# The attention readout's product with the context's low part, cut to two matmuls on 64 rows each

## The reference

```
x = x + xattn(layernorm(x), ctx, mask)
    scores = h @ ctx.T / sqrt(1024), masked; attn = softmax(scores)      # 64 columns
    out    = attn @ ctx                                                  # the readout, 64 x 1024
x = x + ffn(layernorm(x))
    base   = h @ weight.T                                                # 1024 x 1024
    router = softmax(h @ router_w.T), top 2 of 8 experts, renormalized
    out    = base + sum over experts of gate * (h @ lora_A.T) @ lora_B.T * 2
```

## Time and profile before

| | |
|---|---|
| median of 3 runs | 1096.29 us (1095.71 to 1096.64) |
| the profiled execution | 1095.92 us, span 1094.1 us, mean granted TensorE clock 0.994 of full |
| TensorE matmul busy | 1074.6 us, 98% of the span, 6240 matmuls |
| TensorE weight load busy | 1045.9 us, 96% |
| VectorE busy | 789.2 us, 72% |
| ScalarE busy | 466.5 us, 43% |
| GpSimd busy | 114.2 us, 10% |

### The profile page before, as it was taken

How to read it: one execution, slowest core, us unless ns; L and a number is a source line. 1 busy time by engine, 2 the same in 40 slices (tenths; PEclk the granted TensorE clock), 3 DMA queues, 4 the chain that set the end, 5 groups by cost and what they waited for, 6 DMA issues and landing times.

```text
span 1094.1 us, 18329 instructions
## 1 busy us (share of the span) xinstructions
PE 1074.6 (98%) x6240; PEld 1045.9 (96%) x6240; DVE 789.2 (72%) x2047; ACT 466.5 (43%) x954; POOL 114.2 (10%) x282
## 2 busy tenths in 40 slices
PE   7899999999999999999999999999999999999998
PEld 6799999999999999999999999999999999999998
DVE  5867867768677777677777677677776677776663
ACT  5643443443443443443533444434444434434330
POOL 2510010010010010110000100100100100100100
PEclk8999999999999999999999999999999999999999
DMA  9453534643535543544536434445435635345322
GB/s 323 112 164 116 154 84 129 183 136 116 153 81 161 153 123 127 142 115 137 153 105 173 129 95 142 134 147 151 117 95 153 163 116 154 78 133 154 92 64 78
DMA packets 70974, 145.89 MB, mean 133 GB/s; under 512 B 8848, under 2 KB 44176, under 8 KB 70928
## 3 DMA queue, kind: packets, MB, share of 16 engines
q1 hardware_dynamic: 70496, 143.78, 45.6%
q10 hardware_dynamic: 432, 1.57, 0.4%
HBM read 78.74 MB, written 33.55 MB: 103 GB/s over the span
## 4 chain that ended last, share of the span: by engine, by line
DVE 44%; issue 18%; ACT 16%; PE 13%; POOL 7%; DMA 1%; ACTq 1%; POOLq 0%; SPq 0%; DVEq 0%
DVE x2T L698 10%; DVE x L680 7%; DVE stats L686 7%; DVE xT_lo L705 6%; DVE xT_lo L647 6%; ACT xT_hi L451 4%; PE base_ps L836 4%; PE base_ps L838 4%; PE base_ps L837 4%; POOL rstd L384 3%; ACT x2T L437 3%; ACT xT_hi L481 3%; ACT e_all L463 2%; POOL rstd L380 1%; ACT e_split L465 1%
## 5 line engine op out<-in xcount | busy, mean ns | idle before, releaser
L836 PE MATMUL base_ps<-w_hi,xT_hi 128*128 128x388 f32 x1512 | 529.9, 350 | 2.6 <-DVE x L750 1.2
L837 PE MATMUL base_ps<-w_lo,xT_hi 128*128 128x388 f32 x1512 | 511.9, 339 | 0.0
L838 PE MATMUL base_ps<-w_hi,xT_lo 128*128 128x388 f32 x1512 | 511.7, 338 | 0.0
L836 PEld LDWEIGHTS base_ps<-w_hi,xT_hi 128*128 128x128 f32 x1512 | 285.2, 189 | 14.6 <-DVE x L750 4.4
L837 PEld LDWEIGHTS base_ps<-w_lo,xT_hi 128*128 128x128 f32 x1512 | 285.1, 189 | 2.7
L838 PEld LDWEIGHTS base_ps<-w_hi,xT_lo 128*128 128x128 f32 x1512 | 284.2, 188 | 0.0
L475 ACT ACTIVATE xn<-x,shift,rstd 128x1024 f32<-128x1024 f32 x63 | 78.4, 1245 | 313.7 <-POOL shift L387 313.7
L481 ACT CAST xT_hi<-x2T 128x512 fp32r<-128x512 f32 x126 | 72.0, 618 | 129.5 <-DVE x2T L698 129.5
L698 DVE STREAM_TRANSPOSE x2T<-xq 128x512 f32<-128x512 f32 x126 | 126.6, 1081 | 0.0
L384 POOL TENSOR_TENSOR rstd<-var_eps,neg_half 128x1 f32<-128x1 f32 x64 | 36.0, 563 | 688.6 <-DVE var_eps L691 688.6
L705 DVE TENSOR_TENSOR xT_lo<-x2T,xT_hi 128x512 fp32r<-128x512 f32 x126 | 81.4, 687 | 34.8 <-ACT xT_hi L481 34.8
(11 more groups left out here) (98 smaller groups left out, 1159.8 us busy)
## 6 DMA issues: line engine op xcount, KB each, us to landing
out<-x SPq DMA_DIRECT2D x64, 512.0 KB, 3.9
x<-in_x SPq DMA_DIRECT2D x63, 512.0 KB, 3.4
xq<-xn SPq DMA_DIRECT2D x252, 128.0 KB, 3.5
xT_raw<-in_xT SPq DMA_DIRECT2D x62, 512.0 KB, 5.2
ctx_raw<-in_ctx SPq DMA_DIRECT2D x16, 256.0 KB, 5.3
w_raw<-in_wT SPq DMA_DIRECT2D x8, 386.0 KB, 8.2
ctxT_raw<-in_ctxT SPq DMA_DIRECT2D x8, 256.0 KB, 4.6
w_raw<-in_wT SPq DMA_DIRECT2D x4, 388.0 KB, 9.6
```

The lines of the kernel that those rows point to most:

```text
L836: pe.matmul(out_, a_hi, w_h, start=start, stop=False, skip_group_check=again)
L837: pe.matmul(out_, a_hi, w_l, start=False, stop=False, skip_group_check=again)
L838: return pe.matmul(out_, a_lo, w_h, start=False, stop=stop, skip_group_check=again)
```

## The change

The four matmuls of a readout become two over 128 rows (all exponentials by the high context, both halves), and two over 64 rows: the high exponentials alone by the low context. The product of low exponentials and low context is left out. The first of these takes partitions 0 to 63 of `eT` and `ctx_lo` and writes the first half of `ro_ps`; the second takes partitions 64 to 127 and writes the second half. Partitions 64 to 127 of `eT` hold the low exponentials, so ScalarE makes one more copy, `eT_again[64:128]` from `eT[0:64]`, after the first has landed. The order of the four changes from hi, lo, hi, lo to hi, hi, lo, lo, and TensorE waits twice: for the first copy ahead of the four, for the second ahead of the last two. To make room, `ctx_sum` now shares `mask_f`'s memory and `e_all` shares `s_part`'s.

```
-        ctx_sum = sb("ctx_sum", [P, M])
         mask_f = sb("mask_f", [P, M])
+        ctx_sum = mask_f
...
-        e_all = sb("e_all", [P, M])
+        e_all = s_part
...
+        eT_again = sb("eT_again", [P, P], f32r)
...
                 act.copy(eT[:, :], et_ps).then_inc(eT_copied, 1)
+                act.wait_ge(eT_copied, count(tile, 2, 1))
+                act.copy(eT_again[M:P, :], eT[0:M, :].bitcast(f32)).then_inc(eT_copied, 1)
...
-                pe.wait_ge(eT_copied, count(tile, 1, 1))
+                pe.wait_ge(eT_copied, count(tile, 2, 1))
                 for i in range(2):
-
                     pe.matmul(half(ro_ps, i), eT[:, :], half(ctx_hi, i), start=True, stop=False)
-                    pe.matmul(half(ro_ps, i), eT[:, :], half(ctx_lo, i), start=False, stop=True)\
-                      .then_inc(readout_done, 1)
+                pe.wait_ge(eT_copied, count(tile, 2, 2))
+                pe.matmul(half(ro_ps, 0), eT[0:M, :], half(ctx_lo, 0)[0:M, :], start=False, stop=True)\
+                  .then_inc(readout_done, 1)
+                pe.matmul(half(ro_ps, 1), eT_again[M:P, :], half(ctx_lo, 1)[M:P, :], start=False, stop=True)\
+                  .then_inc(readout_done, 1)
```

## The result

The changed kernel took 1101.08 us (median of 5 runs, 1098.95 to 1102.21) against 1096.29 before (1095.71 to 1096.64). The ratio is 1.0043, 95% interval 1.0029 to 1.0058. The measured time lies inside the stated range of 1083 to 1105, but on the other side of no change. Its profiled execution took 1102.21 us, span 1100.4.

A forecast was written before the change was run, and what follows sets the result against it. The prediction took TensorE to bound the kernel: 1095.92 us for the profiled execution, less 6.75 saved in readouts, plus 0.3 at the start, gave 1089.5; with 0.37 to the median, 1089.8 us, 0.6% less, range 1083 to 1105.

The forecast's parts named there:

- the gaps at the two changes of form: TensorE entering and leaving the 64-row pair in each readout: no cost in the forecast.
- tied the second load to the matmul ahead of it: Half-row pair: second load starts with the first half-row matmul, second matmul 0.11 us later; saves 0.125 us per tile.
- Rival 3: Changes between 128 and 64 rows stall TensorE around the pair: 1101.7 us, or 1119 with loads behind; chance 0.26.
- light form: Two TensorE empties of 0.165 us around the pair against 0.235 saved: +0.095 per tile, 1101.7 us; chance 0.14.
- heavy one: Around the pair, the next load also waits after each empty: 0.42 us lost per tile, 1119 us; chance 0.12.
- The argument against a drain: At the transpose and the matmul behind it: 0.11 us of load time explains the whole difference between 0.29 and 0.177.
- TensorE sets the pace: Whole kernel: TensorE, matmuls busy 98% of the span, bounds it; time taken from it mostly comes off the end.
- 54 of 64 readouts count: Savings reach the end except in three start-up readouts and seven at sequence ends: 54 x 0.125 = 6.75 us.
- In the other tiles the waits are VectorE's: Outside the start and sequence ends, VectorE waits for TensorE, so those readouts' savings of 0.125 us each count.
- The second copy: ScalarE's extra copy per tile: 0.27 us, 0.5 us ahead of its reader, covered by idle time ahead of `x2T_high`.
- TensorE's waits at the end of a sequence: At each of seven sequence ends, the one readout's saving is waited away: waits grow by 0.125 us.
- The start: Third tile: the second copy lacks cover and delays `xT_high`, `x2T_high` and `base`, costing 0.3 us once.

The follow-up runs named there:

- e4: The kernel before with the readout's two matmuls by the context's low part left out: 1092.64 us, ratio 0.9975.
- e5: The kernel before with VectorE's low part of the transposed x (xT_low) moved ahead of softmax_split: 1087.15 us, ratio 0.992.
- e2: The changed kernel with the half-row pair issued twice in a row, so the low product is added two times: 1111.66 us, ratio 1.0156.

## Why the prediction was wrong

Two steps failed. The first turned the sign; the second would have taken most of the gain in any case.

**The price of the form.** The prediction took the gaps at the two changes of form as nothing, and tied the second load to the matmul ahead of it. Both were off. The pair starts together (0.235 saved, not 0.125), and each change costs about 0.20 us, 0.40 in all, where the forecast had nothing. Rival 3 had the mechanism and the place right. Its point of decision, 0.118 us per change if the pair starts together, was passed by 0.08. Its light form priced +0.095 per tile and its heavy one +0.42. Measured is +0.161, because emptying takes about 0.09 and not the 0.165 that a record lasts beyond its streaming, and the load is exposed both times. The argument against a drain, that the load time explains the distance around a transpose, says nothing of a change from 128 rows to 64: the transpose and its neighbours are all over 128 rows. That rival's 1101.7 us so near the measured 1101.08 is partly luck: a larger price, half absorbed.

The Trainium skill ("TensorEngine Tiling (Array Packing)", Tiling Modes) says that changing the mode drains the engine; the trace agrees, with the load port idle for 0.36 and 0.25 us beside the pair, and adds the price. The Trainium skill ("TensorE: Matmul & The Clock Gate", Part 3: Packing small matmuls) says that packed matmuls start about 4 ns apart; the trace agrees, 517.38 and 517.39.

**Who sets the pace.** "TensorE sets the pace", so that 54 of 64 readouts count, was wrong, and by more than the first step. Taking 27.7 us off TensorE gave 1.9 (e4), and shortening the other ring alone gave 9.1 in the steady part (e5). Had the pair been free to enter and leave, most of its 0.235 per tile would, by e4, have been waited away in the same manner; no run has such a pair. "In the other tiles the waits are VectorE's" was not so either: in six of them TensorE's load waited ahead of the scores' transpose, 2.6 us. The step failed in reading: 98% busy and VectorE's seventy waits for TensorE were taken as proof that TensorE alone binds. They show only that it is never idle for long. Its short waits in the steady part, some 10 us, show how far it is from being late, but not how soon it would wait if it were faster. The chain that ended last, 44% VectorE and 13% TensorE, was the view for that. A loss passes better than a gain, and here half of it passed.

**The rest.** The second copy was sized well in the steady part: 0.30 us instead of 0.27, done at 516.56, 0.8 us ahead of the pair's loads, and the idle time ahead of `x2T_high` fell from 1.41 to 1.06 us in the same tile. TensorE's waits at the end of a sequence were to grow by 0.125; since the readout got longer, one of them vanished instead. The start was put at +0.3. The fourth readout began at 66.23 us before and at 67.77 after, 1.5 later; in that profile the granted clock was 0.86 and 0.71 in the stretches from 48 and from 52 us, because it stood at the lower of its two levels, 1.2 GHz, for a part of each, where it was 1.00 of 2.4 GHz before. TensorE had been busy 4.00 of 4 us in the stretch from 44, and is busy 2.39 in the one in which the clock falls:

```profile
48.00:52.00 4.00, 2.39 (x12) 1.91 (x11) 3.89 (x10) 2.43 (x8) 0.00 (x0) 0.86 0.30 86
52.00:56.00 4.00, 4.00 (x17) 2.91 (x16) 2.88 (x5) 2.00 (x4) 0.00 (x0) 0.71 0.13 49
```

In the five profiles with the second copy that readout began between 65.31 and 67.99, in the five without between 65.07 and 67.03. Whether the copy itself delays the start by some tenths stays open. `add_readout`'s two waits for `readout_done`, both before 31 us, grew from 0.8 to 1.8 us in all, where the prediction's upper bound for the growth was 0.5.

## What to carry to other kernels

Two half-row matmuls on disjoint rows and banks run fully side by side, but entering and leaving that form costs 0.2 us each way here, so a single pair of 512 columns does not pay. Two pairs in one visit would save 0.47 us against 0.40, an estimate from the costs above that no run tests. Before pricing a saving on an engine that is busy 98% of the span, look at the chain that ended last and follow the ring it takes: where a ring through the other engines is as long as the first engine's own work, a saving on that engine arrives only once the other ring is shortened. Look for it in an in-order engine that waits for an answer while work that needs no answer stands behind the wait; moving that work forward gave 8.6 us here (1087.15 against 1095.73) and beats both kernels.

## What the runs showed of the hardware

- A change between matmuls over 128 and over 64 rows, float32r, at full clock: a little under 0.1 us until the next load starts (517.30 to 517.38, 517.72 to 517.81), and that load's 0.1 us in the open, in either direction, 0.40 us for both. Inside the 64-row form loads are hidden as ever (the second pair's records of e2 last 0.39 us, the first's 0.50).
- Two loads of 64 by 128 for disjoint rows start together (517.38) and are no slower together (0.18 us each) than one of 128 by 128 (0.19).
- The change showed in no semaphore wait. The profile marks such idle time of the load port as "issue".
